# One loop over batches in the attention layer, written out with constant batch numbers

## What is computed

```python
xn = _ln(x, ln_w, ln_b)
q = softmax(heads(xn @ Wq + bq), axis=-1)
k = softmax(heads(xn @ Wk + bk + (1.0 - src_mask) * -1000000.0), axis=1)
v = heads((xn @ Wv + bv) * src_mask)
att = einsum('bnhd,bnhl->bhdl', k, v)
y = einsum('bnhd,bhdl->bnhl', q, att)
hh = silu(_ln(y, ln2_w, ln2_b) * (1.0 + scale) + shift) @ W_out + b_out
x = x + hh
```

## Time and profile before

| | |
|---|---|
| median of 3 runs | 3549.62 us (3545.36 to 3550.64) |
| the profiled execution, its own time | 3546.43 us |
| its span | 3544.6 us |
| granted TensorE clock over the span, of full speed | 0.893 |
| PE busy | 2912.2 us, 82% |
| DVE busy | 2618.2 us, 74% |
| ACT busy | 1469.4 us, 41% |
| POOL busy | 1605.5 us, 45% |
| instructions recorded | 36180 |

### The profile page before, as it was taken

One profiled execution on the slowest core, in us unless ns is written; L12 is line 12 of the kernel. 1 busy time (PEld: TensorE's weight loads), 2 busy tenths in 40 slices (PEclk: granted clock), 3 DMA queues, 4 the chain that ended last, 5 costly groups with the idle time before them and its releaser, 6 DMA issues.

```text
span 3544.6 us, 36180 instructions
## 1 busy us (share of the span) xinstructions
PE 2912.2 (82%) x11066; PEld 1611.0 (45%) x11066; DVE 2618.2 (74%) x3408; ACT 1469.4 (41%) x2028; POOL 1605.5 (45%) x547
## 2 busy tenths in 40 slices
PE   7999999999999985786886886886886886887765
PEld 3545455454554533344444444444444444444432
DVE  3444444444443437999999999999999999999992
ACT  1222122221222215564564564564564565565340
POOL 0121111211111205566586586586586477577671
PEclk9999999999999996977977987987977977978877
DMA  5002021020210321101141141141141141141132
GB/s 189 3 22 77 6 71 53 24 77 0 77 53 24 107 85 36 44 29 39 50 106 39 48 108 37 51 108 36 51 105 39 51 103 41 45 103 49 49 91 60
DMA packets 161656, 211.63 MB, mean 60 GB/s; under 512 B 13293, under 2 KB 78961, under 8 KB 161482
## 3 DMA queue, kind: packets, MB, share of 16 engines
q1 hardware_dynamic: 146152, 183.53, 16.2%
q0 software_dynamic: 11776, 25.17, 3.9%
q10 hardware_dynamic: 3554, 0.88, 0.1%
HBM read 167.32 MB, written 42.22 MB: 59 GB/s over the span
## 4 chain that ended last, share of the span: by engine, by line
DVE 34%; issue 14%; PE 11%; ACT 3%; DVEq 1%; POOL 1%; DMA 0%; POOLq 0%; ACTq 0%
DVE hs L1582 18%; DVE acc L1609 12%; PE bank L1179 4%; PE bank L1162 2%; PE bank L1138 2%; DVE xm L1550 2%; PE bank L1198 1%; DVEq L97 1%; DVE shift L260 1%; PE bank L1168 1%; DVE zs L1615 1%; ACT bank L1357 0%; DVE fin L1626 0%; DVE raw L247 0%; PE bank L1125 0%
## 5 line engine op out<-in xcount | busy, mean ns | idle before, releaser
L1469 POOL TENSOR_TENSOR hs<-u,b_wide 128x2048 f32<-128x2048 f32 x256 | 1171.4, 4580 | 689.8 <-PE bank L1179 579.6
L1582 DVE TENSOR_TENSOR_SCAN hs<-bank,hs 128x512 f32<-128x512 f32 x1024 | 1241.8, 1213 | 19.9 <-ACT bank L1357 12.6
L1179 PE MATMUL bank<-ident,hs 128*128 128x128 f32 x4096 | 766.8, 324 | 382.8 <-DVE hs L1582 265.3
L1357 ACT ACTIVATE bank<-dt,decay 128x512 f32<-128x512 f32 x1024 | 698.1, 689 | 873.8 <-DVE hs L1582 870.5
L1179 PEld LDWEIGHTS bank<-ident,hs 128*128 128x128 f32 x4096 | 569.9, 166 | 947.8 <-issue 478.8
L1609 DVE SCALAR_TENSOR_TENSOR acc<-bank,c_t,acc 128x512 f32<-128x512 f32 x1024 | 745.9, 729 | 50.7 <-PE bank L1179 47.6
L1138 PE MATMUL bank<-h_t,w_in 128*128 128x512 f32 x1024 | 550.7, 626 | 17.3 <-ACT h_t L1288 13.7
L1198 PE MATMUL bank<-w_y,zs 128*128 128x512 f32 x512 | 271.6, 622 | 9.7 <-DVE fin L1626 5.5
L1138 PEld LDWEIGHTS bank<-h_t,w_in 128*128 128x128 f32 x1024 | 178.2, 202 | 112.0 <-issue 99.8
L572 PE MATMUL bank<-z_t,w_k 128*128 128x512 f32 x512 | 221.8, 594 | 5.9 <-ACT z_t L669 5.9
L572 PE MATMUL bank<-w_out,h_t 128*128 128x512 f32 x512 | 221.1, 592 | 0.0
(11 more groups left out here) (152 smaller groups left out, 2946.1 us busy)
## 6 DMA issues: line engine op xcount, KB each, us to landing
w_in<-in_L_cond_W_in SPq DMA_DIRECT2D x128, 256.0 KB, 3.1
b_wide<-b_rows SPq DMA_DIRECT2D x128, 256.0 KB
z<-in_x SPq DMA_DIRECT2D x8, 2048.0 KB, 8.4
res<-in_x SPq DMA_DIRECT2D x8, 2048.0 KB, 8.5
x_rows<-res SPq DMA_DIRECT2D x7, 2048.0 KB, 7.4
fin<-x_rows SPq DMA_DIRECT2D x56, 256.0 KB, 3.5
out<-fin SPq DMA_DIRECT2D x56, 256.0 KB
y_rows<-fin SPq DMA_DIRECT2D x32, 256.0 KB, 3.0
```

Source lines behind the costliest of these rows:

```text
L1179: last = nc.tensor.transpose(state_banks[n % len(state_banks)][:, j * P:(j + 1) * P], hs[:, q % RING, j, t * P:(t + 1) * P], ident[:, :])
L1357: nc.scalar.activation(decay_bank(k)[:, :], dt[:, par, j, :], ACT.Exp, scale=g.decay[:, j, s:s + 1]).then_inc(da_ready, 1)
L1469: nc.gpsimd.tensor_tensor(hs[:, q % RING, :, :], u[:, 4 * half:4 * half + 4, :], b_wide[:, s % 2, :].unsqueeze(1).to_broadcast([P, 4, CHUNK]),
L1582: nc.vector.tensor_tensor_scan(block, decay_bank(k)[:, :], block, 0.0, ALU.mult, ALU.add).then_inc(scanned, 1)
```

## The change

The loop of layer 0 is a Python loop now, so the body is emitted six times for each engine, with b = 1 to 6 as integers. Nothing else in the source changes.

```diff
@@ -504,7 +504,7 @@
             body(0, False, True, True)
-            with eng.Fori(1, BATCH - 1) as b:
+            for b in range(1, BATCH - 1):
                 body(b, True, True, True)
             body(BATCH - 1, True, True, False)
             body(BATCH, True, False, False)
```

## The result

The changed kernel takes 3564.53 us (median of 5 runs, 3563.16 to 3568.39), the kernel before 3549.62 us (5 runs, 3540.73 to 3550.64): ratio 1.0051, 95% interval 1.0037 to 1.0066, slower by 13 to 23 us. The medians are 14.9 us apart and the means 18.2. Run again beside 24 runs of the kernel before, the ratio was 1.0058 (1.0045 to 1.0070). The forecast was 9.15 us. The six bodies of layer 0 cost just that; about as much again, going by the means, came from outside layer 0's loop.

What follows compares the result with a forecast made beforehand. Layer 0 was taken as bound by PE, layer 1 by DVE. Five turns 1.52 us longer and one 1.55 longer gave +9.15 us on the 3549.62 us median, 3558.8 us; stated range 3550 to 3566 us.

Steps and rivals of the forecast that it cites:

- The table load moves behind the wait: Layer 0, bodies 1 to 6: ACT's Silu table load comes after the wait for PE's y transposes; +1.34 us a turn.
- The twin's other differences: Straight body b = 7 against a loop turn: -0.03 us up to the y transposes, +0.19 from Q product to L652.
- Register arithmetic and branches are hidden: Layer 0's loop: removing ALU_OPs gains 0 (at most 13.8 us), removing branches 0.2 us in all (at most 1.4).
- Instruction pages cost nothing in layer 0: Layer 0: some 25 more pages on q8 stall PE by 0; upper bound 22 us.
- Layer 1's code and its timing stay.: Layer 1, bound by DVE, from 1280 us: no change, so nothing in the sum.
- rival D: Layer 1: its code lies elsewhere in memory, so its loop's taken branches cost differently, -3 to +6 us; chance 0.16.
- The time outside the span: Whole execution: span 3544.6 of 3546.43 us in all; no change to the remainder was forecast.
- A: Layer 0, b = 1 to 6: the table load keeps its early place, 3549.6 to 3550.7 us; chance 0.10.
- B: Layer 0's loop: its branch hides a stall, so the change is faster, 3544 us or 3535; chance 0.05.
- C: Layer 0: each straight body waits on PE for one late instruction page, 31 us more, 3581 us; chance 0.05.

Runs made afterwards that it cites:

- dead copies: Kernel before, loop kept, with five more copies of layer 0's body ahead of its loop, branched over and never run: 3556.58 us, ratio 1.0027.
- half a loop: Kernel before with b = 1 to 3 of layer 0 kept as a loop and b = 4 to 6 written out: 3556.63 us, ratio 1.0011.

## Why the prediction was wrong in size

**The table load moves behind the wait.** Right. All eight loads stand there, and PE waits 1.77 us for 0.43. Swapping the waits takes it back, and forcing it into the loop brings it there. Shown.

**The twin's other differences.** Right. 150.30 us a body, the rhythm of the transposes (+0.18) also with the load early (148.96 against 148.78). What makes this rhythm isn't shown.

**Register arithmetic and branches are hidden.** Right: taking them all away left no phase shorter by more than 0.03 us.

**Instruction pages cost nothing in layer 0.** Right, for layer 0. Where the loop had loaded none in four turns, the changed kernel loads 16 pages on q8 from 316 to 917 us (the forecast was some five in each body; it is four), and the V product's 64 records take 27.63 us in body 2, as the Q product's do:

```profile
q8 instruction: 16, 0.26, 0.2%
```

The Trainium skill ("Runtime: NRT & Kernel Launch", "Instruction fetch mechanics") gives the fetch behind a taken branch to a page that isn't at hand as a reason why kernels prefer to be unrolled. Taken as a rule for this loop it would have made the change faster; the measurement decides against it here. In layer 1's loop the trace agrees with it: the branch still costs DVE 2.99 us.

**"Layer 1's code and its timing stay."** This step failed: the sum puts layer 1 at nothing. By the prediction's own sign, over 3 us in the stretch behind layer 0, its rival D was there: the stretch grew by 7.5 us in the first pair of traces. D had a chance of 0.16 and a span of -3 to +6 us, priced by the two branches. The branches themselves didn't change (3.65 and 3.92 us on PE, for 3.72 and 3.96). What came is a second idle time of PE four matmuls behind each of them, 1.84 and 2.06 us, which costs DVE 4.3 us in this pair and which goes when PE's later code is moved by 14 instructions or more. So D's mechanism, that the loop's code lands elsewhere, is borne out, and its size too, but on PE's next instructions and not on the branch. The other 2.8 us or so of the 7.5 lie in the front of layer 1, at a granted clock of 0.75 for 0.79. The clock's spread from run to run was in the prediction only as 5.3 us over three runs; eleven or twelve runs of one kernel lie up to 21 us apart.

**The time outside the span** was taken as a constant 1.8 us, so its change was put at nothing too. It is 1.8 to 1.9 in all ten kernels with the whole loop, the one with dead copies among them, 2.7 with half a loop, and 3.1 to 3.5 in the nine written out. So 1.5 us go with the bodies that are run as straight code. Why stays open; the trace holds nothing there.

Of the prediction's rivals A, B and C nothing was seen in layer 0. The stated range of 3550 to 3566 us holds the first median, 3564.53, but not the second, 3567.94: that the first lies inside is owed to the room left for D, not to the sum, which is 5.7 us below it.

## What to carry to other kernels

Before a loop is written out, look for a body already in straight code: its phases give the price to 0.1 us. Where two waits stand ahead of a ScalarE instruction that needs another function, write the one that is fulfilled last first. Here the wait written second, as a constant, was the one that stood ahead of the table load: with `tr_ready` second the load waited 24.66 us, with `tr_ready` first it came straight behind the Exp of k. Where code ahead of a loop grows or shrinks, look in the traces behind the loop's taken branches for idle time that no wait explains. A ladder of added instructions tells whether it is tied to the code: the idle time moves by as many instructions as were added. And delays made of instructions move the code too, so they can't tell a matter of time from one of place.

## What was not expected of the hardware

The bodies of layer 0 stay loaded on every engine: 512 matmuls and as many weight loads on PE in a turn, and no instruction page on any queue in four turns. A semaphore increment on PE's queue has a row of 51 ns but takes 150 ns from one to the next. A load of one register value and a taken branch at the start of layer 0 made its first stretch 7.7 us longer, 6.02 us of it in PE's branch row. Behind a taken branch PE can idle a second time, 1.56 to 2.09 us, and a shift of the code by four instructions moves that idle time by four. And a stage bound by DVE (2050 of 2197 us busy) still takes part in what PE does: of 17.7 us between two executions, 15.4 were DVE's waits for PE.
